# The gate of a mixture-of-experts router with its weights stationary in four 32-column strips

## What is computed

```python
scores = softmax(xf @ gate_w.T)          # 8192 x 16
# 2 of 4 groups are kept by the sum of their two best scores + gate_b, then the top 2 experts
h  = silu(xf @ We1 + be1) * (xf @ We3 + be3);  y = sum over the 2 experts of weight * (h @ We2 + be2)
z  = silu(xf @ ws1 + bs1) * (xf @ ws3 + bs3) @ ws2 + bs2
x  = x + 0.5 * (y + z)
```

## Time and profile before

| what | value |
|---|---|
| median of 3 runs | 1309.13 us (1305.36, 1309.13, 1309.68) |
| profiled execution: span | 1417.3 us (no separate time of it is given) |
| mean granted TensorE clock | 0.947 |
| busy: TensorE, VectorE, ScalarE, GpSimd | 1238.7, 838.3, 736.0, 696.5 us |
| routing of layer 0 | 24 to some 275 us |
| routed experts of layer 0 | some 290 to 560 us |
| attention, with rounds 8 to 10 | some 590 to 930 us |
| routing of layer 1 | some 920 to 1070 us |
| routed experts of layer 1, final sum | to 1350 us, to 1417 us |

### The profile page before, as it was taken

The page is one execution under the profiler, slowest core; times in us unless marked ns, Lnnn a source line. Parts: engine busy times, 40 slices in busy tenths (PEclk is TensorE's granted clock), DMA queues, the critical chain, the costliest instruction groups (busy, mean ns, idle before and its releaser), DMA issues.

```text
span 1417.3 us, 26677 instructions
## 1 busy us (share of the span) xinstructions
PE 1238.7 (87%) x6864; PEld 982.1 (69%) x6864; DVE 838.3 (59%) x2756; ACT 736.0 (52%) x1700; POOL 696.5 (49%) x849
## 2 busy tenths in 40 slices
PE   4999879799999994999899999999688999999991
PEld 3556556478888883878787787766445988888750
DVE  4576743345565554677858677676532655555567
ACT  3345431056676664565645543544102767676578
POOL 2456754447877775110320412257460777777740
PEclk9999996899999997999989899999899999999996
DMA  9722221745555443111301300012166555554398
GB/s 350 224 72 76 91 79 61 169 132 153 164 158 157 133 136 105 60 60 60 90 31 61 105 30 31 31 61 87 61 150 245 145 159 150 151 151 142 92 350 361
DMA packets 93800, 181.54 MB, mean 128 GB/s; under 512 B 17464, under 2 KB 60240, under 8 KB 91862
## 3 DMA queue, kind: packets, MB, share of 16 engines
q1 hardware_dynamic: 66342, 110.44, 25.5%
q0 software_dynamic: 26016, 67.55, 13.9%
q10 hardware_dynamic: 1296, 1.86, 0.4%
HBM read 97.63 MB, written 86.08 MB: 130 GB/s over the span
## 4 chain that ended last, share of the span: by engine, by line
PE 51%; DVE 15%; ACT 11%; issue 8%; another core or an unknown queue 7%; POOL 5%; DMA 2%; DVEq 0%; ACTq 0%; POOLq 0%; SPq 0%
PE bank L669 16%; PE bank L679 8%; PE bank L532 6%; PE bank L548 4%; POOL expert_rows L1601 4%; PE bank L660 4%; PE bank L509 3%; PE bank L775 3%; ACT w L965 2%; ACT rows L965 2%; PE bank L725 2%; PE bank L701 1%; DVE rows L1381 1%; DVE stat L1106 1%
## 5 line engine op out<-in xcount | busy, mean ns | idle before, releaser
L1664 POOL DMA_INDIRECT routed_rows<-xn,rdest x286 | 282.5, 988 | 175.5 <-issue 79.8
L669 PE MATMUL bank<-rows,att 128*128 128x128 f32 x2288 | 306.1, 277 | 3.3 <-issue 1.5
L669 PEld LDWEIGHTS bank<-rows,att 128*128 128x128 f32 x2288 | 279.9, 193 | 8.4 <-ACT att L954 4.3
L1601 POOL DMA_INDIRECT expert_rows<-rows,slots x160 | 154.9, 968 | 159.0 <-DVE slots L1158 78.5
L1381 DVE SCALAR_TENSOR_TENSOR rows<-bank,tile_b,att 128x128 f32<-128x128 f32 x286 | 99.8, 349 | 170.3 <-ACT att L959 108.4
L679 PE MATMUL bank<-w,rows 128*128 x572 | 178.5, 394 | 18.8 <-DVE rows L1381 16.9
L954 ACT COPY att<-w 128x512 f32 x286 | 179.7, 628 | 10.3 <-issue 6.5
L959 ACT ACTIVATE att<-bank,tile_b 128x128 f32<-128x128 f32 x286 | 107.2, 375 | 110.5 <-PE bank L669 105.4
L548 PE MATMUL bank<-ws,be 128*128 128x256 f32 x512 | 135.7, 416 | 22.3 <-DVE be L1291 22.3
L1394 DVE TENSOR_TENSOR xn<-bank,be 128x256 f32<-128x256 f32 x286 | 121.6, 425 | 38.6 <-issue 22.7
L548 PEld LDWEIGHTS bank<-ws,be 128*128 128x128 f32 x512 | 103.1, 209 | 49.1 <-DVE be L1291 29.2
(11 more groups left out here) (202 smaller groups left out, 2120.6 us busy)
## 6 DMA issues: line engine op xcount, KB each, us to landing
rows<-expert_rows SPq DMA_DIRECT2D x286, 129.5 KB
rows<-routed_rows SPq DMA_DIRECT2D x32, 512.0 KB
w<-routed_rows SPq DMA_DIRECT2D x10, 1024.0 KB, 10.7
w<-in_w SPq DMA_DIRECT2D x2, 4096.0 KB, 18.3
out<-xres SPq DMA_DIRECT2D x16, 512.0 KB, 9.4
xres<-in_x SPq DMA_DIRECT2D x7, 1024.0 KB, 7.5
rows<-routed_rows SPq DMA_DIRECT2D x6, 1024.0 KB, 8.2
expert_rows<-pad SPq DMA_DIRECT2D x47, 129.5 KB
```

The costliest lines, as they stand in the source:

```text
L669: last = nc.tensor.matmul(rh_ps[t % RB][:, n * P:(n + 1) * P], m.rw13[:, t % RB, c * C + n * INTER:c * C + (n + 1) * INTER], m.rT[:, t % R ...
L1601: nc.gpsimd.indirect_dma_start(out=d.xg, out_offset=bass.IndirectOffsetOnAxis(ap=m.slots[:, slots_of(r), k, i:i + 1], axis=0), in_=m.xs[bu ...
L1664: nc.gpsimd.indirect_dma_start(out=d.yt, out_offset=bass.IndirectOffsetOnAxis(ap=m.rdest[:, n:n + 1], axis=0), in_=m.ry[:, n, :], in_offse ...
```

## The change

The gate's weights, padded from 16 to 32 columns, become the stationary operand. They stand in four strips of 32 columns of the array; strip j multiplies the tokens of tiles j and 4 + j, which move as 256 columns. The result has experts on partitions (32 j to 32 j + 31) and tokens in columns. ScalarE copies it to SBUF (128x256, into the space of `tile_b13`), and TensorE turns it back with two 128x128 transposes, into columns 256 to 511 of the same bank, where a tile's logits now stand 32 columns apart.

In the rounds after a layer's first the whole gate is ahead of the first part; the turning back stands in the part after half of its first group of callbacks (after j = 1 of 0 to 3), and ScalarE's copy between the next round's `normalise` and the SiLU of the first part. In rounds 0 and 11 the copy is ahead of the next round's `normalise`. In rounds 8, 9 and 10 the gate moves ahead of the last queries, the copy is between the third `relu_q` and the following normalisations, the turning back behind the last queries.

```diff
-    m.gate_w = sb("gate_w", [P, KC, E])
+    m.scores = m.tile_b13[:, :, :].rearrange("p n t -> p (n t)")[:, 0:2 * P]
+    m.gate_w = sb("gate_w", [P, KC, STRIP])
...
-            def gate(r, i):
+            def gate(r):
                 xnT = m.xnTs[xnT_of(r)]
-                if i == 0:
-                    if early(r - 1):
-                        pe.wait_ge(s.rank_read, r)
-                    pe.wait_ge(s.xT_copied, 4 * r + 4)
-                    wait(pe, s.shift_ready, r)
+                if early(r - 1):
+                    pe.wait_ge(s.rank_read, r)
+                pe.wait_ge(s.xT_copied, 4 * r + 4)
+                wait(pe, s.shift_ready, r)
                 for c in range(KC):
-                    last = nc.tensor.matmul(logits_ps[:, i * E:(i + 1) * E], xnT[:, c, i * P:(i + 1) * P],
-                                            m.gate_w[:, c, :], start=c == 0, stop=c == KC - 1)
-                if i == NT - 1:
-                    last.then_inc(s.logits_ready, 1)
+                    tokens = xnT[:, c, :].rearrange("p (h j n) -> p h j n", h=2, j=STRIPS)
+                    for j in range(STRIPS):
+                        last = nc.tensor.matmul(scores_ps[j * STRIP:(j + 1) * STRIP, :].rearrange("p (h n) -> p h n", h=2),
+                                                m.gate_w[:, c, :], tokens[:, :, j, :],
+                                                start=c == 0, stop=c == KC - 1, tile_position=(0, j * STRIP))
+                last.then_inc(s.scores_ready, 1)
+
+            def turn_scores(r):
+                pe.wait_ge(s.scores_copied, r + 1)
+                for h in range(2):
+                    last = nc.tensor.transpose(logits_at[:, h * P:(h + 1) * P], m.scores[:, h * P:(h + 1) * P], m.ident[:])
+                last.then_inc(s.logits_ready, 1)
...
+                    def turn(j):
+                        if j == 1:
+                            turn_scores(r)
...
-                    shared(L, n, gate_pair)
+                    gate(r)
+                    shared(L, n, turn)
...
                 queries(b, 2)
+                if fresh is not None:
+                    gate(fresh)
                 queries(b, 3)
                 if fresh is not None:
-                    gate_tiles(fresh, range(NT))
+                    turn_scores(fresh)
                 mixer(b)
...
+            def copy_scores(r):
+                act.wait_ge(s.scores_ready, r + 1)
+                nc.scalar.copy(m.scores, scores_ps).then_inc(s.scores_copied, 1)
...
                     n, end = FIRST[L][b - LEAD[L]:b - LEAD[L] + 2]
+                    if b == LEAD[L]:
+                        copy_scores(r)
                     if more:
                         normalise(r + 1)
...
+                    copy_scores(r)
                     shared(L, n)
                     exponentials(r)
...
+            ch.did(nc.gpsimd.memset(m.gate_w[:, :, E:], 0.0))
```

More of the change, by code:

```diff
@@ L26 @@
 E, GROUPS, INTER = 16, 4, 128
+STRIP = 32
+STRIPS = P // STRIP
 PER_GROUP = E // GROUPS
@@ L317, in program @@
     s.xn_half, s.xT_ready, s.xT_copied = sem("xn_half"), sem("xT_ready"), sem("xT_copied")
+    s.scores_ready, s.scores_copied = sem("scores_ready"), sem("scores_copied")
     s.logits_ready, s.shift_ready, s.exp_ready = sem("logits_ready"), sem("shift_ready"), sem("exp_ready")
@@ L349, in program @@
     s.weighted, s.f_weighted = sem("weighted"), sem("f_weighted")
-    ffn_loads = ((m.gate_w[:], d.gate_w), (m.gate_b[:], d.gate_b), (m.ws1[:], d.ws1), (m.ws3[:], d.ws3),
+    ffn_loads = ((m.gate_w[:, :, 0:E], d.gate_w), (m.gate_b[:], d.gate_b), (m.ws1[:], d.ws1), (m.ws3[:], d.ws3),
                  (m.ws2[:], d.ws2), (m.bs1[:], d.bs1), (m.bs3[:], d.bs3))
@@ L359, in program @@
     xT_ps, logits_ps, y_ps, h1_ps, h3_ps = m.bank[0], m.bank[1], m.bank[2:4], m.bank[4:6], m.bank[6:8]
-    logits = logits_ps[:, 0:NT * E].rearrange("p (i e) -> p i e", e=E)
+    scores_ps, logits_at = logits_ps[:, 0:2 * P], logits_ps[:, 2 * P:4 * P]
+    logits = logits_at.rearrange("p (i e) -> p i e", e=STRIP)[:, :, 0:E]
     ranks_at = [bank[:, 0:(NT + 1) * E] for bank in (xT_ps, logits_ps)]
@@ L499, in transpose @@
                 last.then_inc(s.xT_ready, 1)
-            def gate(r, i):
+            def gate(r):
                 xnT = m.xnTs[xnT_of(r)]
-                if i == 0:
-                    if early(r - 1):
-                        pe.wait_ge(s.rank_read, r)
-                    pe.wait_ge(s.xT_copied, 4 * r + 4)
-                    wait(pe, s.shift_ready, r)
-                for c in range(KC):
-                    last = nc.tensor.matmul(logits_ps[:, i * E:(i + 1) * E], xnT[:, c, i * P:(i + 1) * P],
-                                            m.gate_w[:, c, :], start=c == 0, stop=c == KC - 1)
-                if i == NT - 1:
-                    last.then_inc(s.logits_ready, 1)
-            def gate_tiles(r, tiles):
-                for i in tiles:
-                    gate(r, i)
+                if early(r - 1):
+                    pe.wait_ge(s.rank_read, r)
+                pe.wait_ge(s.xT_copied, 4 * r + 4)
+                wait(pe, s.shift_ready, r)
+                for c in range(KC):
+                    tokens = xnT[:, c, :].rearrange("p (h j n) -> p h j n", h=2, j=STRIPS)
[9 more added lines that the diff above has]
+                last.then_inc(s.logits_ready, 1)
             def up(r, u, between):
@@ L597, in route @@
                     more = b + 1 < BATCHES
-                    def gate_pair(j):
-                        gate(r, 2 * j)
-                        gate(r, 2 * j + 1)
+                    def turn(j):
+                        if j == 1:
+                            turn_scores(r)
                     def first_half(j):
@@ L605, in first_half, with turn_and_first_half @@
                             transpose(r + 1, j // 2)
+                    def turn_and_first_half(j):
+                        turn(j)
+                        first_half(j)
                     def second_half(j):
@@ L612, in route @@
                     if b == LEAD[L]:
-                        if L == 0:
-                            gate_tiles(r, range(NT))
                         if L:
-                            shared(L, n, first_half)
+                            shared(L, n, turn_and_first_half)
                             shared(L, n + 1, second_half)
                         else:
-                            shared(L, n)
+                            gate(r)
+                            shared(L, n, turn)
                             shared(L, n + 1)
@@ L836, in _ @@
                 if not more:
-                    gate_tiles(BATCHES + EARLY, range(NT))
+                    gate(BATCHES + EARLY)
             route(1)
@@ L1069, in _ @@
                 relu_q(b, 2)
+                if fresh is not None:
+                    copy_scores(fresh)
                 following(range(4, 6))
```

## The result

The changed kernel takes **1294.84 us** (median of 4 runs, 1292.89 to 1298.76), the kernel before beside it 1309.41 (4 runs, 1305.36 to 1311.14): ratio 0.9896, 95% interval 0.9872 to 0.992. It is faster, by 1.0% or 14 us.

The account below looks back on a forecast made before the run. TensorE, 51% of the last-ending chain, was taken to bound about half the program. Savings of -16.9 and felt stops of +8.2 gave -8.7 us, 1417.3 to 1408.6 in span, carried to the 1309.13 median as 1300, range 1284 to 1320.

Parts of the forecast that it names:

- Gate multiplies, 1.9 us a round: New gate on TensorE in each round: 1.9 us in place of 3.5, with only neighbouring strips overlapping in nine steps of 0.21.
- all four strips at once: Rival for the gate multiplies: all four strips run together, gate 0.89 us, total 1291.5 us; chance 0.17.
- The turn, 0.22: Two transposes on TensorE that turn the scores back, costed at 0.22 us a round.
- The copy, 0.373: ScalarE's 128x256 score copy out of PSUM, 0.373 us each; 0.7 allowed with its two hand-overs.
- Gates that stand alone, -15.4 together: Rounds 0 and 8 to 11: us saved by a shorter gate, an earlier start or a better-held clock.
- the clock of rounds 9 and 10, 3.4 us each: In and behind the gates of rounds 9 and 10: 3.4 us saved in each if the clock stays at 2.4 GHz.
- Clock falls behind the old gate, holds behind the new one: Forecast sign: clock at 1.0 behind the new gates of rounds 9 and 10, where old gates left 0.53 to 0.66.
- Rounds with a queue, +6.75: Rounds 1 to 7 and 12 to 15: rounds 1, 2, 13 at -1.35, -0.5, +0.4, plus felt stops of +8.2 us.
- Of it felt, +8.2: Part of the 38.0 us of TensorE stops before the turn that delays rounds: +2.8, +2.5 and +2.9 in rounds 5, 4, 12.
- The rival of the queue (1322): Rival: the 38 us of stops behind ScalarE's queue are not absorbed and bring back 1.2 GHz; +13, 1322 us; chance 0.14.
- Costed at nothing: One more memset, gate weights landing in 64-byte pieces, and VectorE reading logits at stride 32: no cost.
- Experts' stages unchanged: The two experts' stages, 2 x 260 us, have no gate and were to stay the same.

Follow-up runs that it names:

- the second execution: The kernel before, unchanged, profiled once more as the control for line-by-line comparison: 1307.17 us in its one run, span 1305.3.
- the five rounds alone: New gate and turn only in rounds 0 and 8 to 11, old gate in the other eleven, against the kernel before: 1291.55 us, ratio 0.9858.
- the copy-first kernel: The changed kernel with ScalarE's score copy ahead of the next round's normalisations in every round: 1276.97 us, ratio 0.9759 to the kernel before.

## Why the prediction was right, and where it was not

The forecast of 1300 (1284 to 1320, "faster" 0.52) has the result, 1294.84, in its range. Its two halves were right in sign: the gates that stand alone gain, the rounds with a queue give back. That the total came within 5.2 us is in part luck, because in each half errors cancel.

- **Gate multiplies, 1.9 us a round.** The term furthest off in size. Measured 1.00, which is the rival "all four strips at once" (0.89) and 0.1 more. So a round saves 2.3 us on TensorE, not 1.35. The reason given, that only the second record of one multiply can run beside the next strip's first, fell with the run that orders the gate by strips (1.02). The Trainium skill (TensorE: Matmul & The Clock Gate, Measured speedup vs the span model) pointed to the lower end; sixteen records of 0.22, 3.54 one after another, in 1.00 are 3.5 times with four strips.
- **The turn, 0.22.** Measured 0.22. **The copy, 0.373.** Measured 0.356 as a mean of 16; with hand-overs 0.40 from its start to the turn's (104.48 to 104.88).
- **Gates that stand alone, -15.4 together** (-3 in round 0, -1.5, -4.75 twice, -1.4). Measured -18.6 (-21.5 to -15.6). With the gate at 1.0 the same sum would be 0.9 x 4 + 1.9 lower, -20.9, inside the interval. Within it the clock of rounds 9 and 10, 3.4 us each, was too large: 1.8 as a mean, from the gate made thrice as long. It came from a stretch of 5.86 us at 0.53 and one gate at 0.84, which are round 9's; the second execution's round 9 loses 3.4 us in its records too, of which 2.7 reach the next gate. To give round 10 the same was the error: its gate takes 3.50 (739.97 to 743.47) and loses nothing in itself. The other way, round 8 was given no clock and has 1.0, and round 0 was given 3 and has 4.9 in the traces (23.15 to 38.66 before, 22.80 to 33.40 now, from its gate to the next transposes), nearly all of it the gate, 6.82 against 1.87. "Clock falls behind the old gate, holds behind the new one" is shown: 0.80 and 0.50 against 1.00 and 1.00.
- **Rounds with a queue, +6.75** (-1.35, -0.5, +0.4 and a felt stop of +8.2). Measured +1.4 alone (-0.4 to +3.4), and 5.0 as the difference between the whole change and the five rounds alone. The net was near; its parts were not. The stops came where they were forecast, at 33.3 us against 38.0 + 2.6, but not with these lengths: rounds 4 and 6 stop for 1.98 and 1.95, forecast 6.1 and 8.3. I had laid each stop on the times of one old timeline as if the rounds were independent. Two things were wrong with that. Which scatters are late varies: rounds 3 to 6 there, rounds 3, 4 and 6 in the second execution (round 5 waits 0.91), rounds 3 and 5 in the changed kernel. And a stop cleared in one round comes back in the next, as the run with three of them cleared shows. `rank` was not 2.5 us later either: at 145.21 and 172.44 in rounds 4 and 5, against 152.75 and 172.55 in the second execution.
- **"Of it felt, +8.2."** Too little. With the stops gone the kernel is 18 us faster, not 8. The step that failed is the count of what the rounds would save without them: I gave rounds 3 to 7, 12, 14 and 15 none of their 1.35, in 7 and 15 because of the scatter's start and in the others because the stop or a wait was to set their end. The eleven rounds are worth 13 us. The rival of the queue (1322) had the mechanism right, with TensorE at half pace behind a long stop (105.36 to 108.78), and the price wrong: it counted all 38 us of stops as felt, where taking 33.3 us of them away gave 18.
- **Costed at nothing** (memset, 64-byte pieces, stride of 32): shown, 0.9987. **Experts' stages unchanged**: 218.0 and 217.2 against 220.8 and 218.2, not helped. The 2.8 us in layer 0 can't be put down to the new gate: with the old gate in all rounds the stage takes 220.1.

What stays open: why of 2.3 us saved per round only 1.2 arrive in the copy-first kernel. The waits in layer 0's rounds there (TensorE for copies between transposes and for the selection) and the half pace behind two of them say where, but no run took one of them away.

## What to carry to other kernels

Where a step is split across two engines, look at what stands ahead of the new piece in the second engine's queue: here a copy of 0.36 us behind a normalisation that waits for a scatter cost as much as the faster multiplies brought in eleven of sixteen rounds, and moving it two lines up gave 18 us. Where rounds follow on one another, clearing a wait in some of them may only move it on: the three longest of nine stops cleared gained nothing, the copy half as far back in every round (25.5 us of stops left) gained 11 us, all stops cleared 18. And a chain of small multiplies that stands alone, 32 records of 16 columns under weight loads of 128, costs twice: by its own length, and by the clock of what runs behind it, which a dense form of the same work keeps.

## What the runs showed of the hardware

- Four fp32 multiplies in four 32-column strips of the array run at the same time: sixteen records of 256 columns in 1.00 us from the first start to the next work, 1.02 in the other order of issue; forty-eight in 2.73, so each further four take 0.216.
- The change into and out of strips shows no large cost. The Trainium skill (TensorEngine Tiling (Array Packing), Key Properties) tells of a drain at a change of mode; sixteen records cost 1.00 where four steps of 0.216 are 0.86, so the way in and out can hold some 0.14 us and no more.
- The granted clock stays at 1.00 (2.4 GHz) through 2.7 us of strip multiplies and behind them, where 3.5 to 4.3 us of 16-column multiplies leave it at 0.50 (1.2 GHz) in the 4.4 us behind round 9's.
- The length of an idle stop alone does not tell the clock behind it. In the changed kernel the granted clock is 0.50 for the 3.42 us of work behind the stop of 7.32 us (round 3), 1.00 behind the one of 1.98 (round 4) and 0.51 behind the one of 1.95 (round 6); columns as in the experiments:

```profile
105.36:108.78 3.42, 3.42 (x6) 1.35 (x6) 0.58 (x2) 1.64 (x3) 2.64 (x3) 0.50 0.33 116
...
127.16:130.50 3.34, 3.34 (x14) 2.28 (x13) 2.02 (x6) 0.97 (x1) 1.98 (x3) 1.00 0.11 40
...
178.18:181.50 3.32, 3.32 (x9) 2.68 (x9) 0.00 (x0) 0.89 (x1) 0.00 (x0) 0.51 0.00 0
```
